# A two-layer kernel (diagonal recurrence, then a mixture of experts): statistics of the next tile moved ahead of the projections, and eight adds per tile moved to GpSimd

## What is computed

```python
def recurrence(x, Wd, bd, Wi, bi, gamma, beta):      # x is layernorm(x_in)
    decays = sigmoid(x @ Wd + bd)
    inj = x @ Wi + bi
    h = decays * h + inj                              # scan over the 4096 tokens
    mean, var = moments(states)                       # over the 1024 features
    return (states - mean) * rsqrt(var + 1e-5) * gamma + beta + x
x = x + recurrence(layernorm(x), ...)
x = x + moe(layernorm(x), ...)                        # 8 experts, top 2, d_ff 4096
```

## Time and profile before

| | |
|---|---|
| median of 2 runs | 6078.24 us (5919.81 and 6236.67) |
| the profiled execution | 5909.5 us |
| its span (first to last instruction, slowest core) | 5907.8 us |
| spans of the 8 cores | 5874.2 to 5907.8 us |
| TensorE, VectorE, ScalarE, GpSimd busy | 74%, 29%, 19%, 2% |
| end of the first stage | about 873 us |

### The profile page before, as it was taken

How to read it: one execution, slowest core, us unless ns; L and a number is a source line. 1 busy time by engine, 2 the same in 40 slices (tenths; PEclk the granted TensorE clock), 3 DMA queues, 4 the chain that set the end, 5 groups by cost and what they waited for, 6 DMA issues and landing times.

```text
span 5907.8 us, 49781 instructions; the slowest of 8 cores (5874.2 to 5907.8 us)
## 1 busy us (share of the span) xinstructions
PE 4382.4 (74%) x18678; PEld 1887.6 (32%) x19040; DVE 1685.0 (29%) x2197; ACT 1125.7 (19%) x1429; POOL 120.9 (2%) x167
## 2 busy tenths in 40 slices
PE   1655531988888888888888715989898988889893
PEld 0222110433333333333333312434343333333341
DVE  1344453004040404040404053031404041314135
ACT  0323220202020202020303002130303121221210
POOL 0000000000000000000000000000000000000000
PEclk9877765998999999999999957989899999999896
DMA  5000013655656666666564520314131312222221
GB/s 73 29 29 29 15 34 80 147 147 128 156 127 158 124 161 128 157 126 160 119 166 99 140 71 29 114 59 141 50 121 61 125 70 102 89 96 90 89 89 43
DMA packets 229017, 586.57 MB, mean 99 GB/s; under 512 B 75056, under 2 KB 75184, under 8 KB 220592
## 3 DMA queue, kind: packets, MB, share of 16 engines
q1 hardware_dynamic: 157568, 444.95, 21.8%
q0 software_dynamic: 71216, 138.44, 16.0%
HBM read 570.77 MB, written 150.99 MB: 122 GB/s over the span
## 4 chain that ended last, share of the span: by engine, by line
PE 67%; DVE 15%; DMA 9%; ACT 4%; issue 3%; SPq 1%; DVEq 0%; ACTq 0%; POOLq 0%
PE pall L804 31%; PE pall L853 26%; DMA w2buf<-w 7%; PE pall L414 4%; DVE res_b L862 3%; DVE rs_r L249 3%; ACT sq_b L904 2%; PE pall L913 2%; DMA yacc<-xmid_scr 1%; PE pall L896 1%; SPq L201 1%; DVE xn_b L386 1%; DVE vscr L384 1%; PE pall L939 1%; PE pall L461 1%
## 5 line engine op out<-in xcount | busy, mean ns | idle before, releaser
L853 PE MATMUL pall<-h_b,w2buf 128*128 128x512 bf16 x8020 | 1854.8, 388 | 238.9 <-DMA w2buf<-w 145.5
L804 PE MATMUL pall<-xn_b,w1buf 128*128 128x512 bf16 x8026 | 1853.5, 392 | 143.0 <-ACT h_b L810 65.7
L810 ACT ACTIVATE h_b<-pall,b_c 128x512 bf16<-128x512 f32 x1024 | 703.1, 687 | 3037.7 <-PE pall L804 3036.9
L853 PEld LDWEIGHTS pall<-h_b,w2buf 128*128 128x128 bf16 x8192 | 806.9, 99 | 1286.8 <-issue 394.2
L804 PEld LDWEIGHTS pall<-xn_b,w1buf 128*128 128x128 bf16 x8192 | 818.8, 101 | 1187.7 <-issue 288.1
L862 DVE SCALAR_TENSOR_TENSOR res_b<-pall,b_c,xn_b 128x512 bf16<-128x512 f32 x256 | 192.0, 750 | 2300.4 <-PE pall L853 2276.3
L414 PE MATMUL pall<-xn_b,WdWi_b 128*128 128x512 bf16 x1000 | 244.7, 408 | 206.9 <-DVE x_f L391 78.2
L249 DVE RECIPROCAL rs_r<-rs_r 1x1024 f32<-1x1024 f32 (+1 forms) x30 | 157.8, 5261 | 452.9 <-ACT rs_r L245 452.9
L414 PEld LDWEIGHTS pall<-xn_b,WdWi_b 128*128 128x128 bf16 x1024 | 105.2, 104 | 349.6 <-issue 246.3
L939 PE MATMUL pall<-u_rb,ones_row_b 1*128 1x512 bf16 x64 | 32.9, 614 | 244.4 <-DVE g_rb L932 244.4
L955 DVE SCALAR_TENSOR_TENSOR yacc<-sq_b,fgam_c,yacc 128x512 f32<-128x512 f32 x256 | 192.2, 751 | 29.6 <-DVE sq_b L952 3.7
(11 more groups left out here) (102 smaller groups left out, 1218.6 us busy)
## 6 DMA issues: line engine op xcount, KB each, us to landing
w2buf<-w2s_scr SPq DMA_DIRECT2D x384, 512.0 KB, 4.0
w1buf<-w POOLq DMA_DIRECT2D x32, 2048.0 KB, 18.3
w1s_scr<-w1buf SPq DMA_DIRECT2D x32, 2048.0 KB, 6.4
w2buf<-w POOLq DMA_DIRECT2D x128, 512.0 KB, 8.7
w2s_scr<-w2buf SPq DMA_DIRECT2D x128, 512.0 KB, 6.5
w1buf<-w1s_scr SPq DMA_DIRECT2D x32, 2048.0 KB, 7.9
xt<-ssm_x SPq DMA_DIRECT2D x8, 2048.0 KB, 7.8
xmid_scr<-x_f SPq DMA_DIRECT2D x4, 2048.0 KB, 7.3
```

What stands on the lines that cost most here:

```text
L804: e.matmul(bank(b_), l, rr, start=(kk == 0), stop=(kk == FC - 1)))
L810: e.activation(h_b[:, fo * 1024 + nt * 512: fo * 1024 + nt * 512 + 512], bank(b_), AF.Gelu, bias=b1_c[:, ee * 32 + fo:ee * 32 + fo + 1]))
L853: e.matmul(bank(m2), l, rr, start=(kk2 == 0), stop=(kk2 == 31)))
```

## The change

1. `st_sq` gets a buffer of its own, and `square(k)` no longer waits for the scans of k-1.
2. While k is a prefix tile, the order becomes: tp_evac, stats_sum, square, stats_sq of k+1, then decinj(k) with combine1(k+1) issued between its decay and injection halves and bc1(k+1) behind the fourth injection group; then norm(k+1) and scans(k) (k = 3: scans(3), then norm(4)). Own tiles keep their order.
3. `norm` of own tiles: the product goes to `dec` instead of `vscr`; the 16 operations that yield `xn_b` come first; then, per slice, GpSimd adds the product to `x_f` and VectorE, after waiting for that, adds bank 7. The projections of k wait for the 16 only.
4. `decinj`: ScalarE, before it writes slice m of `dec` or `inj`, waits for scan m of k-1, and before slice m of `dec` also for GpSimd's add m.
5. `post_stats`: TensorE sums the states before, not after, it waits for their squares.

```diff
-    st_sq = dec[:].bitcast(BF16)[:, 0:FC * ST]
+    st_sq = es(nc.sbuf_tensor("st_sq", [128, FC * ST], BF16))
 def square(k):
-        r.wait("s", tk.get(("scanall", k - 1)))
 def norm(k):
+        fc_tok = [None] * FC
         for fc in range(FC):
             sl = slice(fc * ST, (fc + 1) * ST)
-            r.emit("v", lambda e, sl=sl, xf=xf: e.tensor_tensor(
-                vscr[:], xf[:, sl], bank(6), ALU.mult))
-            r.emit("v", lambda e, sl=sl: e.tensor_tensor(
-                xn_b[:, sl], vscr[:], bank(7), ALU.add))
-            if own:
-                r.emit("v", lambda e, sl=sl, xf=xf: e.tensor_tensor(
-                    xf[:, sl], xf[:, sl], vscr[:], ALU.add))
-                r.emit("v", lambda e, sl=sl, xf=xf: e.tensor_tensor(
-                    xf[:, sl], xf[:, sl], bank(7), ALU.add))
+            scr = dec[:, sl] if own else vscr[:]
+            r.emit("v", lambda e, sl=sl, xf=xf, scr=scr: e.tensor_tensor(
+                scr, xf[:, sl], bank(6), ALU.mult))
+            r.emit("v", lambda e, sl=sl, scr=scr: e.tensor_tensor(
+                xn_b[:, sl], scr, bank(7), ALU.add))
+            fc_tok[fc] = r.token("v")
         v = r.token("v")
         tk[("norm", k)] = v
         bank_free[6] = v
-        bank_free[7] = v
         if not own:
+            bank_free[7] = v
             tk[("xfg", par)] = [v, tk[("summ", k)]]
+            return
+        qtok = [None] * FC
+        for fc in range(FC):
+            sl = slice(fc * ST, (fc + 1) * ST)
+            r.wait("q", fc_tok[fc])
+            r.emit("q", lambda e, sl=sl, xf=xf: e.tensor_tensor(
+                xf[:, sl], xf[:, sl], dec[:, sl], ALU.add))
+            qtok[fc] = r.token("q")
+            r.wait("v", qtok[fc])
+            r.emit("v", lambda e, sl=sl, xf=xf: e.tensor_tensor(
+                xf[:, sl], xf[:, sl], bank(7), ALU.add))
+        tk[("wacc", k)] = qtok
+        bank_free[7] = r.token("v")
 def decinj(k, mid=None, mid2=None):
                 r.wait("s", mm_t)
-                if which == 0 and m == 0:
-                    r.wait("s", tk[("sqmm", k)])
+                r.wait("s", tk.get(("scanfc", k - 1), [None] * FC)[m])
+                if which == 0:
+                    r.wait("s", tk.get(("wacc", k), [None] * FC)[m])
...
                 bank_free[b_] = r.token("s")
+                if which == 1 and m == 3 and mid2 is not None:
+                    mid2()
+            if which == 0 and mid is not None:
+                mid()
 def post_stats(k):
-        r.wait("t", bank_free[3])
         r.wait("t", tk[("scanall", k)])
-        r.wait("t", tk[("psq", k)])
         for fc in range(FC):
...
+        r.wait("t", bank_free[3])
+        r.wait("t", tk[("psq", k)])
         for fc in range(FC):
 for k in range(n_tiles), prefix tiles:
+                tp_evac(k + 1)
+                stats_sum(k + 1)
+                square(k + 1)
+                stats_sq(k + 1)
+                decinj(k, mid=lambda k=k: combine1(k + 1),
+                       mid2=lambda k=k: bc1(k + 1))
+                if k + 1 >= N_SST // 2:
+                    scans(k)
+                    norm(k + 1)
+                else:
+                    norm(k + 1)
+                    scans(k)
```

## The result

| | before | after |
|---|---|---|
| ratio after / before | | **0.9803**, 95% interval 0.9789 to 0.9818 |
| median of all runs | 6180.89 us (10 runs) | 5802.68 us (11 runs) |
| profiled execution | 5909.5 us | 5802.7 us (forecast 5800) |
| first stage, median core | 758.2 us | 644.1 us |
| window behind the first stage, slowest core | 5029.8 us | 5033.1 us |

The change makes the kernel 2.0% faster, and that is some thirteen times the half-width of the interval.

What follows compares the result with a forecast made beforehand. The prediction took a chain of hand-offs, with no engine full, to bound the first stage; 69.0 + 19.0 + 14.8 + 7 = 110 us off 5909.5 gave 5800, range 5775 to 5845.

Steps and rivals of the forecast that it cites:

- the one at 0.04: GpSimd's adds in the own tiles' norm cost so much that the kernel gets slower; 6043 us at 10 us per add; chance 0.04.
- Hand-offs, not a full engine, bound the first stage: First stage, about 107 to 873 us: no engine is full, so a chain of hand-offs sets its time.
- Term 1: Prefix tiles 0 to 3 reordered, period 54.3 against 69.2, and tile 4's norm shortened: D(4), its projections, starts 69.0 us sooner.
- Term 2: Norm of own tiles 5 to 7: eight adds move from VectorE to GpSimd, 6.3 us sooner in each, 19.0 in all.
- Terms 3 and 4: post_stats, four own tiles: state sums start 3.7 us sooner each, 14.8; those sums at a held high clock, 7 more.
- term 4: State sums in post_stats: the shorter idle of 2.7 us may keep TensorE's clock high; 10.0 us if so, 7 taken.
- The second stage shifts whole: The 5,030 us behind the first stage run the same code and start when it ends, so they only move earlier.
- A slow GpSimd: Own tiles' norm: GpSimd's add (price P) takes about 3.3 us, VectorE idles, 30 us lost, 5830; chance 0.12.
- The engines block each other: norm(4) to norm(7): each GpSimd add lengthens the norm by at least 0.69 us, 22 in all, 5822; chance 0.08.
- Slower by P over 5.8: Own tiles' norm: a GpSimd add price P of 5.8 us eats the whole 110 us gain; chance 0.04.
- A fuller overlap: Prefix tiles: the sums of k+2 don't wait for the norm, four times 11.3 us less, 5755; chance 0.04.

Runs made afterwards that it cites:

- the experiment with the banks: Changed kernel with the statistics of tiles 0 to 4 summed into banks 2 and 3 instead of 6 and 7: first stage 610.1 us, -34.0 against the changed kernel.

## Why the prediction was right, and where it was wrong

The time was right (5800 against 5802.7, ratio forecast 0.9815, measured 0.9803 in 0.9789 to 0.9818), and so was the mechanism. **The verdict built on it was wrong.** I gave 0.63 to a change of less than 2%, which I took for one that can't be told from none, and 0.33 to faster by more. The kernel is faster clear of all noise, and its 0.9803 lies on the 2% border itself, too close to say on which side. That the two times agree to 3 us is in part luck: the stage shortened by 114.1, 4 more than the sum of the terms, and the difference of the two executions came out 7 below that.

**The step that failed is the one that turned 110 us into chances.** The prediction said that 2% (5791) is "about what a measurement of this kernel can tell from none". The interval measured here is 0.15% to either side, some 9 us. My own range, 5775 to 5845, lay wholly below the 5909.5 of before, so by my own cases the kernel was faster in all but the one at 0.04; I laid the border through the middle of my forecast and put the larger part on the side of no change. The right reading of the same terms was: faster, by 1.9%.

Point by point, in the order of the prediction:

- **Hand-offs, not a full engine, bound the first stage.** Right. The three parts act on three different hand-offs and add up, 113.7 against 114.1.
- **Term 1, 69.0.** The first of the two things in it, the new order, was 56.0 (forecast 69.0 - 12.7 = 56.3); the other, tile 4's shorter norm, 12.5 (12.7). The pieces fell as written: sums behind the norm, 1.15 of stall at the broadcast (1.1), D(0) at 160.1 (159.4), D(4) at 371.5 (369.1). The period was 54.8, not 54.3, and the excess lies in D, which takes 30.6 (214.9 to 245.5 for D(1)) where I had 30.0; the norm with its hand-offs took 12.9 (12.97), both sums together 11.2 to 11.4 (11.3).
- **Term 2, 19.0.** 19.7. GpSimd's price, bounded by 0.69 and 3.34, was 1.27 and lay on the side I took. By the Trainium skill, GPSIMD Engine Reference, section 3.1, my estimate was 1.1 us; the trace has 1.27 for 512 elements, a little more.
- **Terms 3 and 4, 14.8 + 7.** 25.5 alone, 21.8 forecast. The term that was mis-sized is term 4: I counted 7 of 10 us, because the clock in the gap of the kernel before had fallen within the first 3 us. In the profiled execution of the changed kernel it did not fall in any of the four tiles on any core (L477's mean is 592 ns on all eight, that of the high clock). Windows of the changed kernel show both kinds of gap; the granted clock is third from the end.

```profile
196.80:200.00 3.20, 0.00 (x0) 0.00 (x0) 2.78 (x5) 3.11 (x1) 0.00 (x0) 0.79 0.81 262
200.00:203.50 3.50, 0.00 (x0) 0.01 (x1) 2.98 (x6) 0.50 (x1) 0.00 (x0) 0.50 0.93 324
203.50:209.00 5.50, 5.48 (x7) 0.86 (x8) 5.11 (x4) 0.00 (x0) 0.00 (x0) 0.51 0.06 22
...
401.70:404.30 2.60, 0.01 (x1) 0.00 (x0) 1.98 (x3) 0.69 (x1) 0.00 (x0) 1.00 0.00 0
404.30:411.50 7.20, 7.14 (x18) 1.51 (x19) 0.00 (x0) 3.62 (x1) 0.00 (x0) 1.00 0.00 0
```

  Behind the norm TensorE has idled 7.4 us, stands at 0.50 (1.2 GHz) and the first sums run so. Before the sums of the states it idled 2.66 and stays at 1.00 (2.4 GHz).
- **The second stage shifts whole.** Right: from the end of the first stage on, the median core took 5020.9 and 5019.3 us in the two executions, single cores from 5000.5 to 5034.6 and from 4997.0 to 5038.3.
- **Rivals.** A slow GpSimd (P of 3.3): out, 1.27. The engines block each other: out, 0.69 us beside GpSimd's adds even with twice the work on it; the Trainium skill, SBUF — State Buffer, section "SBUF: two separate sides", names VectorE instructions with two SBUF inputs among those that share a port with GpSimd, and the norm, with one, was not held up, which agrees; a case with two was not tried. Slower by P over 5.8: out. A fuller overlap: out for this kernel, bank 6 holds; but its price, four times 11.3, was wrong too, as the experiment with the banks showed: 34, because transposes and sums are 15.1 us of TensorE in a row.

What the profile of the two executions alone would have hidden: their difference is 106.8 us, while the stage shortened by 114.1. The slowest core of the one was core 6, of the other core 2; spans of the cores of one execution differ by 34 and 42 us. The 7 us are the choice of core: from core 6 of the one to core 2 of the other the stage is 110.9 us shorter (756.5 and 645.6), and what follows it is 3.7 longer (5034.6 and 5038.3).

## What to carry to other kernels

Price a change by the hand-off that it shortens, and ask for each engine's list what stands in front of the instruction that everyone waits for: here eight short activations per tile in the wrong place of ScalarE's list cost nearly as much in three tiles (51.5 us) as a whole reordering of four tiles brought (56.0). When a wait is removed, sum the work that is left on the engine itself before you count the wait as gain: 15.1 us of TensorE were waiting behind a norm of 12.7. And hold a forecast of some per cent against the scatter of repeated runs of one kernel, not against a round border.

## What the runs showed of the hardware that I had not expected

- A two-input f32 add of 128 x 512 takes 1.27 us on GpSimd if it writes over one of its inputs in this kernel, and 1.04 us when both inputs are the same tile and the output another (L402 and L405 above). Why was not tried.
- An idle gap of the same length can keep the clock or lose it. TensorE idled 2.66 us ahead of the sums of the states in the changed kernel, in the one with post_stats only and in the one with the prefix sums in banks 2 and 3. In the changed kernel all 32 groups (four tiles, eight cores) ran at 2.4 GHz, 7.03 us each. With post_stats only, 28 did. With the prefix sums in banks 2 and 3, 26 did; tiles 4 and 5 took 8.5 to 8.7 us on three cores, behind the same gap. The windows of one of the three at tile 4 (core 1; the granted clock third from the end) show the clock fall as the sums begin:

```profile
364.50:366.70 2.20, 0.00 (x0) 0.01 (x1) 1.53 (x3) 0.38 (x2) 0.00 (x0) 0.96 0.00 0
366.70:369.00 2.30, 2.28 (x3) 0.36 (x4) 0.00 (x0) 2.30 (x1) 0.00 (x0) 0.50 0.00 0
```

  So the discount in term 4 was not unreasonable, but what it should stand for is a loss of some 1.5 us in some groups at this length of gap; what decides which is open. Gaps of 5.7 to 7.4 us, in the kernel before and the changed one, lost the clock each time, at 1.4 to 2.8 us a group.
